# One stacked weight input for each expert: two transfers with other rows in a fused attention and mixture-of-experts kernel

## The reference, cut to what matters

```python
gx = xp[buf_tok]                                    # (64, 128, 512): 128 rows for each expert
gu = jnp.einsum('ech,ehi->eci', gx, gate_up_proj)   # weights 64 x 512 x 384
g, u = jnp.split(gu, 2, axis=-1)
hid = jax.nn.silu(g) * u
eo = jnp.einsum('eci,eih->ech', hid, down_proj) * buf_w[..., None]   # weights 64 x 192 x 512
routed = zeros.at[buf_tok.reshape(-1)].add(eo.reshape(-1, h))
shared = jax.nn.silu(xf @ shared_gate_w.T) * (xf @ shared_up_w.T) @ shared_down_w.T
```

## Time and profile before

| | us |
|---|---|
| runs without the profiler, median of 3 (lowest, highest) | 1178.17 (1174.67, 1179.82) |
| the profiled execution: its own time | 1176.7 |
| the profiled execution: its span | 1174.8 |
| stage C in it, from the first weights of the ring's second round to the end | 740.7 to 1174.8 |

### The profile page before, as it was taken

The page is one execution under the profiler, slowest core; times in us unless marked ns, Lnnn a source line. Parts: engine busy times, 40 slices in busy tenths (PEclk is TensorE's granted clock), DMA queues, the critical chain, the costliest instruction groups (busy, mean ns, idle before and its releaser), DMA issues. The chain is left out here.

```text
span 1174.8 us, 17631 instructions
## 1 busy us (share of the span) xinstructions
PE 1091.5 (93%) x5113; PEld 853.6 (73%) x5113; DVE 841.1 (72%) x1444; ACT 529.2 (45%) x958; POOL 714.1 (61%) x414
## 2 busy tenths in 40 slices
PE   3999999999999999999789999999899899899873
PEld 2777777787777877777678888777677676677542
DVE  3799999999999999998589973555555555465443
ACT  5565556655566555653322222444344344343331
POOL 6999999999999999991300002245444353543433
PEclk9999999999999999999799999999999899999987
DMA  6365554455544555442694345799999999999984
GB/s 188 105 183 157 156 164 134 136 153 156 162 134 134 156 156 165 137 126 62 140 279 117 107 115 161 208 289 279 284 248 287 248 264 282 245 285 256 274 207 52
DMA packets 92029, 217.08 MB, mean 185 GB/s; under 512 B 11239, under 2 KB 16167, under 8 KB 91856
## 3 DMA queue, kind: packets, MB, share of 16 engines
q1 hardware_dynamic: 75440, 177.75, 50.1%
q0 software_dynamic: 16544, 38.78, 16.0%
HBM read 164.82 MB, written 52.18 MB: 185 GB/s over the span
## 5 line engine op out<-in xcount | busy, mean ns | idle before, releaser
L1058 POOL TENSOR_TENSOR ring<-vT,pT 128x1024 f32<-128x1024 f32 x128 | 249.4, 1959 | 9.3 <-ACT vT L802 9.1
L444 PE MATMUL Y<-split,toep 128*128 128x512 f32 x576 | 238.0, 413 | 12.1 <-ACT toep L796 9.3
L1066 POOL TENSOR_TENSOR split<-ring,split 128x1024 fp32r<-128x1024 f32 x96 | 231.1, 2407 | 1.5 <-ACT split L808 1.5
L446 PE MATMUL Y<-split,toep 128*128 128x512 f32 x576 | 227.0, 394 | 0.0
L445 PE MATMUL Y<-split,toep 128*128 128x512 f32 x576 | 225.7, 392 | 0.0
L688 PE MATMUL Y<-ring,xT 128*128 128x384 f32 x512 | 197.7, 511 | 0.0
L1212 DVE TENSOR_TENSOR z<-Y,cT 128x1024 f32<-128x1024 f32 x128 | 157.0, 1226 | 26.6 <-PE Y L448 25.5
L1218 DVE TENSOR_REDUCE o<-z 128x128 f32<-128x1152 f32 x128 | 172.1, 1345 | 1.2
L1105 POOL DMA_INDIRECT stage<-xn_rows,idx_i x64 | 73.5, 1149 | 159.6 <-issue 159.6
L444 PEld LDWEIGHTS Y<-split,toep 128*128 128x128 f32 x576 | 108.8, 189 | 32.1 <-issue 10.2
L808 ACT ACTIVATE split<-ring 128x1024 fp32r<-128x1024 f32 x96 | 100.8, 1050 | 57.7 <-POOL ring L1058 57.7
(11 more groups left out here) (165 smaller groups left out, 1884.2 us busy)
## 6 DMA issues: line engine op xcount, KB each, us to landing
ring<-_L_ffn_gate_up_proj_dram SPq DMA_DIRECT2D x64, 768.0 KB, 6.0
ring<-in_L_ffn_down_proj_dram SPq DMA_DIRECT2D x64, 384.0 KB, 8.0
gr<-filters SPq DMA_DIRECT2D x32, 512.0 KB, 4.1
stage<-in_x_dram SPq DMA_DIRECT2D x32, 256.0 KB, 5.4
pT<-in_turned_dram SPq DMA_DIRECT2D x32, 256.0 KB, 4.3
cT<-in_turned_dram SPq DMA_DIRECT2D x32, 256.0 KB, 4.2
xr<-in_x_dram SPq DMA_DIRECT2D x32, 256.0 KB, 3.7
xn_rows<-xn SPq DMA_DIRECT2D x32, 256.0 KB, 2.9
```

Source lines behind the costliest of these rows:

```text
L444: pe.matmul(y, high, kv[:, s, 0, a, n], start=(a == 0), stop=False)
L446: last = pe.matmul(y, low, kv[:, s, 0, a, n], start=False, stop=(a == c))
L1058: pool.tensor_tensor(to.rearrange("p (b j i) -> p b j i", i=NH, j=NH), a, d, ALU.mult).then_inc(kvp_ready, 1)
L1066: pool.tensor_tensor(kv[:, s, 1, c, :], kvp[c], kv[:, s, 0, c, :].bitcast(F32), ALU.subtract).then_inc(kv_ready, 1)
```

## The change: one input with other rows

The host stacks the weights of an expert into one array `expert_rows`: first 96 rows of 10240 bytes (the 6144 bytes of gate and up weights of partition p, then the 4096 bytes of down weights of partition p), then 32 rows of 6144 bytes (the gate and up weights of partitions 96 to 127). The kernel still issues two transfers for an expert at the same places: the first fills partitions 0 to 95 of the buffer over its whole width, the second partitions 96 to 127 over the first 1536 numbers. Every number lands where it did; the semaphore counts, the waits and all other engines' instructions are the same.

```diff
         def weights(sp, e, r):
 
-            sp.dma_start(ring[:, r, 0:NC * SI],
-                         gate_up[e].rearrange("(p c) n -> p (c n)", p=P)).then_inc(weights_in[r], 16)
-            sp.dma_start(ring[0:IH, r, NC * SI:],
-                         down[e].rearrange("(p c) n -> p (c n)", p=IH)).then_inc(weights_in[r], 16)
+            whole = IH * (NC * SI + 2 * L)
+            sp.dma_start(ring[0:IH, r, :], expert_rows[e, 0:whole].rearrange("(p n) -> p n", p=IH)).then_inc(weights_in[r], 16)
+            sp.dma_start(ring[IH:P, r, 0:NC * SI], expert_rows[e, whole:].rearrange("(p n) -> p n", p=P - IH)).then_inc(weights_in[r], 16)
...
+def expert_rows(gate_up, down):
+
+    up = gate_up.reshape(E, P, NC * SI)
+    whole = np.concatenate([up[:, 0:IH], down.reshape(E, IH, 2 * L)], 2)
+    return np.concatenate([whole.reshape(E, -1), up[:, IH:].reshape(E, -1)], 1)
```

More of the change, by code:

```diff
@@ L55, with build @@
 NY = 4
-def build(nc, x, skip, ctx_in, k, gate_w, gate_up, down, sh_gate, sh_up, sh_down,
-          c_sq, c_order, c_slot, ctx_turned, out):
+def build(nc, x, skip, ctx_in, k, gate_w, sh_gate, sh_up, sh_down,
+          c_sq, c_order, c_slot, ctx_turned, expert_rows, out):
     xn_rows = nc.dram_tensor("xn_rows", [T + CAP, LP], F32, kind="Internal").ap()
@@ L1582, in _ @@
             c_result_a(E // 2 - 1)
-_INS = ['x', 'fside_S2_0', 'ctx_2048', 'L0_xattn_k', 'L0_ffn_gate_w', 'L0_ffn_gate_up_proj', 'L0_ffn_down_proj',
+_INS = ['x', 'fside_S2_0', 'ctx_2048', 'L0_xattn_k', 'L0_ffn_gate_w',
         'L0_ffn_shared_gate_w', 'L0_ffn_shared_up_w', 'L0_ffn_shared_down_w']
@@ L1614 @@
     data.append(("turned", turned(_np.asarray(inputs["ctx_2048"]))))
+    data.append(("expert_rows", expert_rows(_np.asarray(inputs["L0_ffn_gate_up_proj"]), _np.asarray(inputs["L0_ffn_down_proj"]))))
     for name, value in data:
```

## The result

The changed kernel takes 1241.39 us (median of 4 runs, 1231.58 to 1246.43), the kernel before 1176.42 in the runs beside it (1172.32 to 1179.82). The ratio is 1.0522, with a 95% interval of 1.0482 to 1.0562. It is slower, as forecast, but by 65 us and not by 21, above the range, which ended at 1223. All times, medians and ratios here are of runs in the faster of the chip's two states; one of the six runs of `h1_two_transfers_rows_2560` was in the slower one and is left out.

A forecast was written before the change was run, and what follows sets the result against it. Bound: nearly full DMA engines delaying adds and gathers, so TensorE waits. 60 x 0.58 = 35 us of engine time less 14 us idle gave 21 us, so 1195.8 us of span and 1199 us forecast; range 1161 to 1223 us.

The forecast's parts named there:

- The bound: Last 15 of 40 slices: full DMA engines delay adds and gathers, so TensorE waits; about 31 us lost.
- The chain of adds: GpSimd's adds each wait for earlier adds to land, median 7.5 us; gathers queue behind them, delaying TensorE.
- rhythm of 12.22 us a pair: TensorE's undisturbed beat for a pair of experts in the last 15 slices, forecast to stay at 12.22 us.
- the 27 pairs: Expert pairs from 740.73 to 1101.50 us: 360.77 us, against 329.9 at TensorE's own beat.
- The slow rate for 96 partitions: First weights transfer: 10240-byte packets at the down rows' 18 bytes/ns, 0.569 us each; case's chance 0.44.
- The 32 rows: Second weights transfer, partitions 96 to 127: 0.246 us a row taken, 7.9 us in all; from above 15.7 us.
- The upper end: Second weights transfer at double cost: 1.06 us more engine time for an expert, 50 us in all, 1228 us.
- The 14 us of cover: Engines idle 3.8% of 370 us from 760 to 1130 us; 14 us taken off the added 35 us.
- longer turns on the engines: Rival: long weights packets delay each add's packets, some 23 us less 8; about 1193 us; chance 0.14.
- Stage B: Stage where four experts' weights are loaded, used 130 us later; costed at nothing.
- stage C: Last 15 of the 40 slices, where 60 experts' weights load; 35 us more engine time claimed.
- The ring's lead: Weights buffer filled four experts ahead, some 24 us; hides later landings, costing only beyond about 20 us.

The follow-up runs named there:

- h1_two_transfers_rows_2560: Weights zero-padded to 128 partitions, against the kernel before; two transfers for an expert, each of two 2560-byte pieces for a partition: 1161.79 us, ratio 0.9846.
- e8_down_cut: Kernel before with the down transfer of experts 4 to 63 cut to 512 bytes for a partition: 1146.92 us, ratio 0.9743.
- e1_up_96_32: Kernel before with the gate and up transfer cut into partitions 0 to 95 and 96 to 127, row lengths kept: 1214.35 us, ratio 1.0295.
- e9_up_64_64: Kernel before with the gate and up transfer cut into two of 64 partitions each, row lengths kept: 1228.58 us, ratio 1.043.
- e2_padded_128x10240: Against the changed kernel, zeros added on partitions 96 to 127; one transfer of 128 rows of 10240 bytes for an expert: 1187.91 us, ratio 1.007.
- e10_after_short_rows: Changed kernel with its 10240-byte rows cut into two transfers of 96 rows of 5120 bytes: 1216.73 us, ratio 1.0341.
- f3_after_rows_2560: Changed kernel with its 10240-byte rows cut into four transfers of 96 rows of 2560 bytes: 1196.61 us, ratio 1.0148.
- e4_down_on_128: Kernel before with the down rows padded with zeros from 96 to 128 partitions: 1177.14 us, ratio 0.9995.

## Why the prediction was wrong in size

**The bound** held. The chain of adds stretches, the gathers behind it come late, and TensorE waits (69.7 us for 26.1), at an unchanged rhythm of 12.22 us a pair. Of the 53.8 us lost in the 27 pairs it stood still for some 42; the other 12 are slower products behind the waits, for which the sum had no term of their own. Relief gives back 32 us and no more (`e8_down_cut`).

**The slow rate for 96 partitions** was the right mechanism. `e1_up_96_32` and `e9_up_64_64` show it with packets of unchanged length, and `e2_padded_128x10240` shows that length has hardly a part in the rate (24 bytes/ns, against 25 in the earlier trace rows). Its size was too small: 0.645 us a packet for 0.569, 246 GB/s for 272.

**The 32 rows** were mis-sized too. I took the low end for them, 0.246 us, "as there are only two of them to an engine"; they took 0.39 us in the mean. By the means, the long rows (0.634 us) cost 0.39 us more for an expert than I had, the 32 rows 0.29, and 0.23 of that stand in the kernel before as well (3.56 us where I had 3.33). By the queue's share, the engine time of an expert rose by 0.99 us and not by 0.58, which is 25 us for 60 experts, the largest part of the miss. The upper end that I had worked out, 1.06, was nearly right: 60 x 0.99 - 14 = 45 us. The estimate by the Trainium skill's page "SBUF — State Buffer", section "Door 1: The DMA port swizzle (why `[64,N]` ≈ `[32,N]`)", took that end and came to 1228 us.

**The 14 us of cover** is the second step that failed. I took them off because the engines had idled that long, and called only the rest uncovered. From 760 to 1130 us both queues together held the engines for 62.0 + 34.9 = 96.9% of the time, where it was 96.2%: 11.5 us stayed idle of 14.1. So the added engine time came almost whole, 54 experts x 0.99 = 53.5 us, and the 27 pairs did take 53.8 us longer. `e1_up_96_32`, with rows of 6144 and 4096 bytes, did use its idle time, 99.5% over the same stretch:

```profile
q1 hardware_dynamic: 14851, 61.89, 63.5%
q0 software_dynamic: 12352, 29.51, 36.0%
...
ring<-_L_ffn_gate_up_proj_dram SPq DMA_DIRECT2D x51, 576.0 KB
```

There the engine time of an expert rose by 0.635 x 370 / 51 - 3.69 = 0.92 us, 50 us for 54 experts, and the 27 pairs (743.02 to 1137.59) took only 33.8 us more. `e10_after_short_rows` and `f3_after_rows_2560` stand at 99.7 and 99.6%, `e9_up_64_64` at 101.2 (the records overlap a little).

**The cost beside engine time** is the same failure from the other side. I had "longer turns on the engines" as a rival in which the rates do not differ, and never added it to the slow rate. It does add. Against `e9_up_64_64` the changed kernel has no more engine time and is 13 us slower. `f3_after_rows_2560`, on the same partitions with short rows and more transfers, is 45 us faster, of which its engine time (4.40 us for an expert against 4.68) explains 17. That the idle time which the long rows leave unused is this cost rests on one profile of each form. In the order in which one can edit, 62 of the 65 us divide into 35 us for cutting the gate and up rows at 96 (`e1_up_96_32`), and 27 us for joining the down rows to them; the other 3 are the kernel before, 1176.42 us beside the changed kernel and 1179.18 beside `e1_up_96_32`.

**Stage B** I costed at nothing; the first issue of stage C came 7.2 us later. SyncE's store of a tile of the shared expert starts at 589.86 us before and 589.85 after, and the store four tiles later at 620.99 and 627.15. So the delay arises while the weights of the first four experts are loaded (587 to 612 us) and just behind. Other forms have their first issue of stage C from 739.5 to 744.9 us, those with 96 and 32 or 64 and 64 partitions from 743.0 up, but two padded ones too. One profile each doesn't tell how much of the 7 us is the change's.

As an estimate from these rows, 60 x 0.99 = 59.4 us of engine time, less 2.6 us of idle time used, and 7.2 us in stage B make 64.0 of the 64.8 us.

**The ring's lead** hid nearly all of the later landings, as said; TensorE waited 2.8 us for weights.

**Open**: why more transfers help at a fixed packet and equal engine time (23 us at 2048 bytes), and why two transfers do as well as four at 2560. The Trainium skill ("DMA: Bandwidth & Descriptors", "Queues, rings and completion order") says that an engine changes between queues at packets of several descriptors, so its turns are not the one row each of my rival's sum. A turn would then be a piece of a transfer's share on an engine, larger than one row, and could shrink with both row length and transfer. The table fits that in part, but no record here shows an engine's order. Five transfers are also issued over some 2 us and not at once; whether that spacing does it was not tried. Nor was any of it tried on a kernel with other sizes.

## What to carry to other kernels

Where the DMA engines are full, count engine time and not bytes or packets: padded with zeros to all 128 partitions a ninth more bytes cost nothing here (`e4_down_on_128`), while the same weights on 96 and 32 partitions cost 38 to 53 us. Don't take idle engine time off an added load before you know that the load can use it. Where a latency-bound chain on another queue shares the engines with a bulk stream, try to cut the stream into short rows and several transfers; five transfers of 128 rows of 2048 bytes beat both kernels (1153.18 us, 0.9809 of the kernel before). And when two mechanisms of a forecast point the same way, ask whether they add before making them rivals.

## What the hardware did that I had not expected

- The same 6144-byte packets took 0.246 us in a transfer onto 128 partitions and 0.374 us in two of 64. Packets of 10240 bytes took 0.425 us onto 128 and 0.645 onto 96.
- At equal engine time for an expert (3.69 us) the time differed by 9 us, and a form with more engine time (3.83 us, 2560-byte rows) was 20 us faster than the kernel before. The DMA share of the page is no measure for what a queue's stream costs the others.
- 640 pieces of 2048 bytes cost 23 us more in one transfer than in five, at the same engine time; pieces of 2560 bytes cost the same in two and in four.
- Behind a wait of 10.90 us TensorE ran at a granted clock of 0.50 until 932 us, and four turns took 1.09 us instead of 0.60. In the 27 pairs this made its products 11.7 us longer, on top of 42.3 us more of standing still.
